# Third layer's attention in row and column tiles of the array, with row sums from a ones column, the mask on TensorE, the experts' tokens stationary and the rotation folded into the query weights

## The reference, cut to what matters

```
q = (xn @ Wq.T)  16 heads of 16;  k, v = xn @ Wk.T, xn @ Wv.T   one head of 16, shared
q = apply_rope(q) over the HEAD index (b, t, h, d -> positions are heads); k: position 0, unchanged
scores = einsum('bhqd,bokd->bhqk', q, k) * D ** -0.5, causal mask over 256 tokens
probs  = softmax(scores);  s = einsum('bhqk,bokd->bhqd', probs, v) -> [t, 256] @ Wo.T
ffn: 16 experts, the 4 best per token, at most 128 tokens per expert,
     (silu(x @ w_gate[e]) * (x @ w_up[e])) @ w_down[e], widths 256 -> 176 -> 256,
     plus a shared expert of width 352
```

## Time and profile before

| what | value |
|---|---|
| three runs, us | 1130.98, 1133.09, 1135.73; median 1133.09 |
| profiled execution, us | 1132.91, of which the span from first to last instruction is 1130.8 |
| granted TensorE clock over the span | 0.941 of 2.4 GHz |
| third layer: `route_stage` | 507.6 to 582.8 us |
| third layer: `attention_and_expert_stage` | 582.85 to 769.97 us |
| busy over the span | PE 89%, DVE 67%, ACT 44%, POOL 34% |

### The profile page before, as it was taken

The page is one execution under the profiler, slowest core; times in us unless marked ns, Lnnn a source line. Parts: engine busy times, 40 slices in busy tenths (PEclk is TensorE's granted clock), DMA queues, the critical chain, the costliest instruction groups (busy, mean ns, idle before and its releaser), DMA issues. The chain is left out here.

```text
span 1130.8 us, 14811 instructions
## 1 busy us (share of the span) xinstructions
PE 1009.8 (89%) x4900; PEld 662.8 (59%) x4900; DVE 757.7 (67%) x1218; ACT 499.3 (44%) x1135; POOL 380.9 (34%) x284
## 2 busy tenths in 40 slices
PE   5799856894999999849989989996899989999997
PEld 4355543353566566545468868885666657555554
DVE  3689973335999999767738868827566640765762
ACT  3543222365988788244134434433566641111112
POOL 0389900006888788520011222210355540000000
PEclk9899977895999999988889999987999999999999
DMA  4112113004000000022022333371000000111001
GB/s 119 39 61 93 42 44 129 0 3 111 19 19 29 20 19 11 1 54 70 1 90 58 87 86 76 89 219 57 1 1 2 1 1 15 42 32 53 28 0 38
DMA packets 53917, 52.55 MB, mean 46 GB/s; under 512 B 10088, under 2 KB 48840, under 8 KB 53856
## 3 DMA queue, kind: packets, MB, share of 16 engines
q1 hardware_dynamic: 50256, 47.05, 14.0%
q0 software_dynamic: 3072, 4.20, 2.2%
q10 hardware_dynamic: 528, 0.52, 0.1%
HBM read 44.19 MB, written 5.47 MB: 44 GB/s over the span
## 5 line engine op out<-in xcount | busy, mean ns | idle before, releaser
L1001 POOL TENSOR_TENSOR seen<-state,c_row 128x512 f32<-128x512 f32 x128 | 160.7, 1278 | 39.0 <-PE banks L1136 27.6
L1020 DVE TENSOR_TENSOR_SCAN state<-decay,banks 128x512 f32<-128x512 f32 x128 | 155.5, 1217 | 20.3 <-issue 7.3
L2279 PE MATMUL banks<-xnT,weight 128*128 128x512 f32 x256 | 115.0, 592 | 1.0 <-PEq L2006 1.0
L2013 POOL TENSOR_TENSOR prob<-prob,inverse 128x512 f32<-128x512 f32 x64 | 65.3, 1042 | 109.0 <-DVE inverse L2098 109.0
L960 ACT ACTIVATE weighed_x<-dx_tok,b_tok 128x512 f32<-128x512 f32 x128 | 90.2, 710 | 24.8 <-PE banks L1122 24.5
L1122 PEld LDWEIGHTS banks<-ident,weighed_x 128*128 128x128 f32 x512 | 59.4, 142 | 64.0 <-ACT weighed_x L960 42.0
L970 ACT ACTIVATE decay<-delta_pairs,A 128x510 f32<-128x510 f32 x128 | 90.6, 707 | 6.2 <-DVE state L1020 6.2
L1122 PE MATMUL banks<-ident,weighed_x 128*128 128x128 f32 x512 | 81.0, 282 | 6.9 <-ACT weighed_x L960 6.0
L2320 DVE TENSOR_TENSOR inter<-gelu,banks 128x512 f32<-128x512 f32 x32 | 22.0, 687 | 96.7 <-ACT gelu L2311 96.1
L2311 ACT ACTIVATE gelu<-banks 128x512 f32<-128x512 f32 x32 | 19.1, 597 | 138.1 <-PE banks L2279 138.1
L2279 PEld LDWEIGHTS banks<-xnT,weight 128*128 128x128 f32 x256 | 48.6, 190 | 49.3 <-issue 47.8
(11 more groups left out here) (363 smaller groups left out, 2047.3 us busy)
## 6 DMA issues: line engine op xcount, KB each, us to landing
prob_row<-probs_dram SPq DMA_DIRECT2D x8, 512.0 KB, 4.1
c_row<-c_dram SPq DMA_DIRECT2D x32, 128.0 KB, 2.8
slot_gate_w<-in_L_ffn_w_gate SPq DMA_DIRECT2D x16, 176.0 KB
slot_up_w<-in_L_ffn_w_up SPq DMA_DIRECT2D x16, 176.0 KB
slot_down_w<-in_L_ffn_w_down SPq DMA_DIRECT2D x16, 176.0 KB
gate_up_w<-in_L_ffn_gate_up_w SPq DMA_DIRECT2D x8, 256.0 KB, 4.2
delta_pairs<-conv_in SPq DMA_DIRECT2D x8, 256.0 KB, 3.4
w_WqT<-in_L_attn_W_q SPq DMA_DIRECT2D x1, 2048.0 KB, 10.1
```

The lines of the kernel that those rows point to most:

```text
L1001: nc.gpsimd.tensor_tensor(seen[:, u % ring, :], state[:, u % ring, :], c_row[:, v % 4, :], ALU.mult).then_inc(seen_ready, 1)
L1020: nc.vector.tensor_tensor_scan(state[:, u % ring, :], decay[:, u % ring, :, :].rearrange("p b t -> p (b t)"), banks[:, 4 + u % 2, :], 0.0, ...
L2013: nc.gpsimd.tensor_tensor(prob[:, u % 2, h, :, :], prob[:, u % 2, h, :, :], inverse[:, u % 2, h, :].unsqueeze(2).broadcast_to([P, 2, SEQ]) ...
L2279: last = nc.tensor.matmul(banks[:, 4 + 2 * half + j, :], weight[:, s, j, k, tile * P:(tile + 1) * P], xnT[:, k, cols[half]], start=(k == 0 ...
```

## The change: what it does

In `route_stage` the rotation moves into the query weights: POOL multiplies `Wq` by `cos` and `Wq_swap` by `sin` (both now rows of 256 values, sent to all partitions, with the softmax scale in them) and adds them, and a `q` job is one product that ACT only copies. `keys` has two copies instead of eight: even and odd heads, zero in the other 16 rows of each 32. `v` becomes 32 columns wide: 16 values, a column of ones, zeros.

In `attention_and_expert_stage` four units form a group, one for each 32 rows of the array. `score(g)` issues four (or eight) matmuls of 32 rows, one for each tile and bank, then four bf16 matmuls of the identity with the mask, which add the mask to the four banks. DVE takes the maximum straight from the bank, negated. `weigh(g)` has the 32 columns of `v` stationary in four column tiles, and `probT` moving. The ones column gives the row sums; ACT copies the bank to `o_raw`; `spread_sums` (PE) copies each head's sum to its 16 rows; DVE `invert` takes the reciprocal of all 512 columns; POOL `divide` multiplies. `mix` multiplies with `Wo` (spread over four blocks with zero rows) inside the loop, once a sequence. The experts' tokens are stationary in `widen`, with gate and up weights as one moving operand of 352 columns; `turn_mid` and `copy_mid` turn the result for `lower`. The loop is written out, 48 steps and a tail, with an expert begun every 2.5 steps; the last expert is lowered at step 40.

All results that go through PE's transposes, the sums, the mix, and the lowered tokens take turns in two banks (4 and 5). `begin_turn` waits until the turn two places before has been emptied, by DVE or by ACT. The four score banks are rewritten only when the whole group's `exps` are done.

```diff
-    dve_ends = [kind in "qs" for kind, _, _ in jobs]
+    dve_ends = [kind == "s" for kind, _, _ in jobs]
...
+                pool.wait_ge(*late_weights)
+                for name, factor in (("Wq", "cos"), ("Wq_swap", "sin")):
+                    nc.gpsimd.tensor_tensor(w[name][:, :, :], w[name][:, :, :],
+                                            w[factor][:, :].unsqueeze(1).broadcast_to([P, KD, D]), ALU.mult
+                                            ).then_inc(q_turned, 1)
...
+                        pe.wait_ge(q_turned, 3)
-                    wide = {"k": ("Wk", "Wk"), "q": ("Wq", "Wq_swap"), "s": ("sw_gate", "sw_up")}[kind]
+                    wide = {"k": ("Wk", "Wk"), "q": ("Wq",), "s": ("sw_gate", "sw_up")}[kind]
...
-                        for h in range(8):
+                        for h in range(2):
                             nc.scalar.activation(keys[:, h, :], krep[:, :], ACT.Identity, scale=w["head_rows"][:, h:h + 1])
...
+    first_wide = [(5 * e) // 2 - 1 for e in range(EXPERTS2)]
+    def sums_at(step):
+        g = step // group - 1
+        return [2 * (g // 3) + (g % 3) // 2] if step % group == 1 and 0 <= g < groups and g % 3 != 1 else []
+    for step in steps:
+        if 0 <= step < units:
+            turns.append(("prob", step))
+        turns += [("sum", n) for n in sums_at(step - 2)]
+        turns += [("mix", n // 2) for n in sums_at(step - 4) if n % 2]
+        turns += [("x", e) for e in experts_at(step, 0)]
+        turns += [("mid", e) for e in experts_at(step, 3)]
+        turns += [("low", e) for e in experts_at(step, 4)]
+    on_vector = [kind in ("prob", "sum", "low") for kind, _ in turns]
...
+                def begin_turn(kind, i):
+                    n = turn_of[kind, i]
+                    if n >= 2:
+                        turn_emptied(pe, *turns[n - 2])
+                    return turn_bank(kind, i)
+                def score(g):
+                    b, kind, _ = part_of(g * group)
+                    if g:
+                        pe.wait_ge(prob_ready, g * group)
+                    for j, kd in enumerate(pairs):
+                        for r in range(group):
+                            tile = slice(r * rows, (r + 1) * rows)
+                            nc.tensor.matmul(banks[:, r, 2 * j * n_keys:2 * (j + 1) * n_keys], q[tile, kd, first:first + P],
+                                             keys[tile, :, b * SEQ:b * SEQ + n_keys], start=(j == 0), stop=False,
+                    for r in range(group):
+                        nc.tensor.matmul(
+                            banks[:, r, :].rearrange("p (h k) -> p h k", h=heads)[:, :, n_keys - P:], ident_bf[:, :],
+                            later_bf[:, :].unsqueeze(1).broadcast_to([P, heads, P]), start=False, stop=True,
+                            skip_group_check=True).then_inc(scored, 1)
+                def weigh(g):
+                    turn_emptied(pe, "prob", g * group + group - 1)
+                            out = banks[r * rows:(r + 1) * rows, 6, :]
+                                last = nc.tensor.matmul(out, v[:, 2 * b, :], probT[:, u % 8, :], start=True, stop=True,
+                def spread_sums(n):
+                    nc.tensor.matmul(bank, w["sum_rows"][:, :], o_raw[:, n % 2, :], start=True, stop=True).then_inc(turned, 1)
+                def widen(e):
+                    if e:
+                        pe.wait_ge(mid_ready, e)
+                    for k in range(KD):
+                        last = nc.tensor.matmul(banks[:, 7, 0:2 * WIDE2], xgT[:, e % 2, k * P:(k + 1) * P], wide_w[:, e % 2, k, :],
+                                                start=(k == 0), stop=(k == KD - 1))
...
+                def invert(n):
+                    turn_done(dve, "sum", n)
+                    if n >= 2:
+                        dve.wait_ge(oT_ready, n - 1)
+                    nc.vector.reciprocal(inverse[:, n % 2, :], turn_bank("sum", n)).then_inc(vector_emptied, 1)
...
+                for step in steps:
+                    if 0 <= step < units:
+                        keep_turned(step)
+                        if step % group == group - 1 and step + 1 < units:
+                            for u in range(step + 1, step + 1 + group):
+                                top(u)
+                    for n in sums_at(step - 2):
+                        invert(n)
+                    for e in experts_at(step, 2):
+                        middle(e)
+                    for e in experts_at(step, 4):
+                        weigh_result(e)
...
+                    late = step % group == group - 1
+                    for e in experts_at(step, 3):
+                        copy_mid(e)
+                    if late and 0 <= step + 1 < units and step >= 0:
+                        exps(step + 1)
```

More of the change, by code:

```diff
@@ L1497, in attention_and_expert_stage, with part_of @@
     w_gate, w_up, w_down = expert_w
-    pairs = EXPERTS2 // 2
-    group = 4
-    seq_units = 3 * HEADS2 // group
-    round_ = 2 * seq_units
-    rounds = BATCH // 2
-    turns = round_ // 3
-    assert turns * rounds == EXPERTS2
-    scale = HEAD2 ** -0.5
+    rows = 32
+    group = P // rows
+    units = BATCH * 3 * group
+    groups = units // group
+    first_wide = [(5 * e) // 2 - 1 for e in range(EXPERTS2)]
+    def part_of(u):
+        return u // group // 3, u // group % 3, u % group
@@ new lines, in spread_sums, with mix @@
+                def spread_sums(n):
+                    pe.wait_ge(o_raw_ready, n + 1)
+                    bank = begin_turn("sum", n)
+                    nc.tensor.matmul(bank, w["sum_rows"][:, :], o_raw[:, n % 2, :], start=True, stop=True).then_inc(turned, 1)
+                def mix(b):
+                    pe.wait_ge(oT_ready, 2 * b + 2)
+                    bank = begin_turn("mix", b)
+                    for t in range(2):
+                        for j in range(4):
+                            last = nc.tensor.matmul(bank[:, t * D:(t + 1) * D], oT[:, j, (2 * b + t) * P:(2 * b + t + 1) * P],
+                                                    w["Wo"][:, j, :], start=(j == 0), stop=(j == 3))
+                    last.then_inc(turned, 1)
@@ new lines, in turn_mid, with lower @@
+                def turn_mid(e):
+                    pe.wait_ge(mid_ready, e + 1)
+                    bank = begin_turn("mid", e)
+                    for part in range(2):
+                        last = nc.tensor.transpose(bank[0:ROWS2, part * P:(part + 1) * P],
+                                                   mid[:, e % 2, part * ROWS2:(part + 1) * ROWS2], ident[:, :])
+                    last.then_inc(turned, 1)
+                def lower(e):
+                    turn_emptied(pe, "mid", e)
+                    pe.wait_ge(down_loaded[e % 2], DMA * (e // 2 + 1))
+                    bank = begin_turn("low", e)
+                    for part in range(2):
+                        last = nc.tensor.matmul(bank[:, 0:D], midT[:, e % 2, part * P:(part + 1) * P],
+                                                down_w[:, e % 2, part, :], start=(part == 0), stop=(part == 1))
+                    last.then_inc(turned, 1)
@@ new lines, in _ @@
+                score(0)
+                for step in steps:
+                    if 0 <= step < units:
+                        turn(step)
+                        if step % group == group - 1 and step + 1 < units:
+                            score(step // group + 1)
+                    if step % group == 1 and 0 <= step // group - 1 < groups:
+                        weigh(step // group - 1)
+                    for n in sums_at(step - 2):
+                        spread_sums(n)
+                    for n in sums_at(step - 4):
+                        if n % 2:
+                            mix(n // 2)
+                    for e in experts_at(step, 0):
+                        turn_tokens(e)
+                    for e in experts_at(step, 1):
+                        widen(e)
+                    for e in experts_at(step, 3):
+                        turn_mid(e)
+                    for e in experts_at(step, 4):
+                        lower(e)
@@ L1794, in weigh_result @@
                         dve.wait_ge(scattered, DMA * (e - 1))
[L1795 to L1814 removed]
+                    nc.vector.tensor_scalar(result[:, e % 2, :], turn_bank("low", e)[:, 0:D], slot_weight[:, e:e + 1],
+                                            None, ALU.mult).then_inc(vector_emptied, 1)
```

474 lines of the change are left out of this document (206 added, 268 removed).

## The result

The changed kernel takes **1157.7 us** (median of 4 runs, 1156.8 to 1159.1) against 1133.5 before (1131.0 to 1135.7): 1.021 of before, 95% interval 1.020 to 1.023. Slower by 24 us, where 10 was forecast. The direction holds, and the time lies within the wide range (1114 to 1166 us), but 2.7 us beyond the forecast's own range (1136 to 1155), and the size is more than twice what was forecast.

A forecast was written before the change was run, and what follows sets the result against it. The prediction took the chain of waits between engines, with DVE's reciprocals on it, to bound the second stage: 162 + 9 + 27.9 - 187.1 = +11.8, with -1.7 about +10, so 1143 us (own range 1136 to 1155, wide 1114 to 1166).

The forecast's parts named there:

- loop, walk: Second stage's loop, engine by engine at full clock: the last turn begins 162 us after the stage's start, against 156.7.
- loop, half clock: Second stage's loop: PE's idle waits put parts at 1.2 GHz, adding 9 us, about 2.5 for a sequence's two long waits.
- end part: From the last unit's turn to the next layer: 27.9 us instead of 30.4.
- norm's and first stage: Query jobs halve in the first stage; two of four lie behind PE's wait, 3.4 us less, half taken: -1.7.
- upper bound, 20 us: Most the lower clock could add in the second stage's loop: 20 us, at 0.87 on average, all on the chain.
- The first sequence: Start of the second stage's loop, one reciprocal in the chain: 36 us, by the same method as the second sequence.
- The reciprocal's price and place: DVE's inverse of 512 columns costs 3.25 to 3.3 us, behind four tops and ahead of the next copy; PE waits.
- the tiles: Scores and weighs in the second stage: four tiles run fully side by side, 0.85 us a group's score, plus shape changes.
- DVE's sum: DVE's work in the second stage comes to 105 us, 26 of it for eight reciprocals.
- That slack also covers ... more weights to load: First stage: PE's 1.7 us idle before `chosen_ready` also absorbs POOL's three products and the added weight loads.
- the forecast's signs: Trace checks for the second stage, such as reciprocal 3.2 to 3.3 us, PE idle behind it, clock at or under 0.93.
- The rival of a cheap reciprocal: Second stage: 512 columns invert at about a copy's cost, each 2.6 us less, total 1109 us; chance 0.14.

The follow-up runs named there:

- kernel 4: The changed kernel with 10 unread matmuls on PE after each spread of the sums and none ahead of the scores: 1142.4 us, ratio 1.007 to before.
- kernel 3: The changed kernel with 13 unread matmuls on PE after each spread of the sums and 3 ahead of each group's scores: 1150.6 us, ratio 1.014 to before.
- kernel 1: The changed kernel with DVE copying the sums instead of inverting them, the inverse left out: 1120.3 us, ratio 0.990 to before.
- kernel 9: The changed kernel with four of its loads issued in the first stage instead of at the norm's stage's end: 1152.3 us, ratio 1.016 to before.
- kernel 7: The changed kernel with the experts' part alone undone (weights stationary again, no turn or copy of the result): 1153.3 us, ratio 1.017 to before.

## Why the prediction was right in direction and wrong in size

The forecast had +10, the profiled executions differ by 24.2. By its own terms:

| Term | forecast, us | measured, us |
|---|---|---|
| loop, walk | 162 | 160 to 165 at full clock, estimated (below) |
| loop, half clock | 9 | 21.8 beyond the walk |
| end part | 27.9 | 27.4 |
| norm's and first stage | -1.7 | -0.7 (with 0.7 us by which the norm's loads already start later) |
| after the second stage | 0 | +0.8 |

- **The step that failed is "I take 9" for the clock.** The walk's own distances hold where the clock was full: 7.85 us from turn 15 to 16 (7.8), 11.1 for units 12 to 15 (11.0). Units 16 to 19 took 19.1 instead of 17.2, with 3.4 us of the weigh and the mix at half clock (1.7), and units 20 to 23 took 18.5 instead of 15.9, with 6.9 us at half clock, in which PE was busy for 5.6 (2.8). The forecast gave 2.5 to a whole sequence; the second had 4.5. Its upper bound, 20 us, was near the truth, and less than half of it was chosen without a row behind the choice.
- What shows it: kernel 4 took 15.8 us off PE's slow work and the loop gave 13.7, 87%. If all 24.6 us go by the same share, the clock is 21 us and the walk is left with 162. That step is an extrapolation, the 13.7 is measured, and two other estimates lie around it. In kernel 3 the second and third sequence, at a clock of 1.00, took 47.0 us each; less 1.25 us of delay at each of two waits that is 44.5, where 44 was walked. Its whole loop less seven such delays is 165. Kernel 1's loop is 151.9; less the 10.3 by which PE's work exceeds 117.2, plus the 18.6 of the reciprocals, it is 160. So the walk was right to some 3 us, and the clock's part is 19 to 24 us against the 9.
- Why it is so much: beyond its own length the wait costs through the work behind it. When the inverse arrives PE has turns, a weigh, a mix and an expert queued, on the chain; in the group shown the clock fell to 0.50 within 2 us of the wait's end, and the weigh and a part of the mix ran at 1.2 GHz. Shorter waits alone raise the clock (kernel 1). The Trainium skill, TensorE: Matmul & The Clock Gate, HAM oscillation — how this bites in real kernels, counts the cost of waits for DMA in a loop of matmuls as the time at the low clock times (1 - 1.2/2.4). An estimate by that page makes of the loop's 57.7 us at half clock 28.9; the trace has 24.6 by PE's busy time, since PE was idle for part of it, and the loop lost no more than that.
- The first sequence, walked by analogy with 36, took 43.4. Its first 9.6 us, with PE busy for 7.9, were at half clock, and so were 10.3 us later with PE busy for 9.6: 17.5 us of slow work, worth 8.7, which would cover the missing 7.4. Kernel 3 still had 40.3 there, which less one delay of 1.25 is 3 us over the walk; but its clock was 0.91 in that sequence, and 1.00 in the others. How much of the 3 us is the clock's and how much the analogy's isn't settled.
- **The reciprocal's price and place were right** (3.35 us; 22.1 + 4.5 us of PE's waits), and so were the tiles: eight passes in 1.07 us, which is 0.85 and one change of shape as the forecast reads them; no run parts the two. The Trainium skill, TensorE: Matmul & The Clock Gate, Measured speedup vs the span model, has 3.07 for four row tiles of 512 columns; here one by one would be 3.4 us, so 3.2. DVE's sum, 100.5 in the loop and 4.6 behind it, is the forecast's 105.
- **The first stage came near by two errors that offset each other.** "That slack also covers ... more weights to load" was wrong: the loads stand on SP's queue at the end of the stage ahead, where each costs 0.4 to 1.1 us of issue and every engine waits; 11.4 us instead of 9.3. Behind it, the stage got 3.5 us shorter rather than 1.7: the two query jobs gave 1.8 (5.2 us instead of 6.95), the rest came elsewhere in the stage.
- Of the forecast's signs, the reciprocal's length, PE's wait behind it and the clock under 0.93 came true. The turns of units 23 and 35 lie 50.6 us apart, not 44 to 48, and the next layer comes 211.2 us after the stage's start, not 197 to 200, both for the clock's sake. The rival of a cheap reciprocal falls by its 3.35 us; its own terms add up to 1107, not 1109.
- The end part was right as a sum; the mix took 5.9, not 7.0 (a part of it at full clock), and the other links 0.7 more.

## What to carry to other kernels

When a change puts a wait of some microseconds on PE's chain, price the work that PE does behind it at half clock too; here this cost some 20 us on top of 27 us of waits, and 2 us of useless matmuls in each wait gave 15 us back. A row operation whose cost goes by columns (a reciprocal at 6.5 ns each) belongs in the layout with the fewest columns, even if PE has to turn it twice. And a load added to a stage may cost its issue on the queue, however long its data has time.

## What the runs showed of the hardware that was not expected

- An f32 matmul of 128 columns shows two rows and takes 0.21 us; an f32 transpose of 128 columns shows one and takes 0.107.
- SP's issues took 0.43 to 0.47 us for most of the loads in a row, but in the changed kernel 1.76 for two, 1.13 and 0.65 for the last four of 19; in the kernel before the last two of 18 took 0.98 together. In kernel 9, with 15, the slow issues came at the start of the next stage instead (3.57 for two).
- The first stage, with the same code, took 70.7 us in the trace of kernel 7 (at a clock of 0.84), 71.8 in that of the changed kernel (0.86), and 75.8 and 76.7 in those of kernels 4 and 3 (0.79 both). So one trace against another tells a few microseconds only where positions within a stage are compared; the profiled execution of kernel 4 is 7.1 us shorter than the changed kernel's, while the medians differ by 15.
